# Routed experts in three split float32r terms, with weights as the moving operand

## The reference, cut to what matters

```python
scores = sigmoid(h @ gate_w.T)                       # 1024 x 16
topk_score, topk_ids = top_k(scores.T, cap)          # each of 16 experts takes cap = 128 tokens
xin = h[topk_ids]                                    # 16 x 128 x 512
up = einsum('ecd,efd->ecf', xin, up_w) + up_b[:, None, :]      # F = 2048
g  = einsum('ecd,efd->ecf', xin, gw) + gb[:, None, :]
eo = silu(g) * up
eo = einsum('ecf,edf->ecd', eo, down_w) + down_b[:, None, :]
out = zeros_like(h).at[topk_ids].add(eo * topk_score) + shared(h)
```

## Time and profile before

| | |
|---|---|
| median of 3 runs | 3031.3 us (3031.16 to 3031.32) |
| profiled execution | 3031.67 us, of which the trace's span is 3029.8 us |
| PE busy | 2971.4 us, 98% |
| DVE, ACT busy | 1830.8 us, 60%; 1361.5 us, 45% |
| last block, first to last matmul | 2335.88 to 3019.83 us |
| its step | 10.58 us |
| its DMA, 2400 to 2900 us | busy share 0.80, 306 GB/s |

### The profile page before, as it was taken

The page is one execution under the profiler, slowest core; times in us unless marked ns, Lnnn a source line. Parts: engine busy times, 40 slices in busy tenths (PEclk is TensorE's granted clock), DMA queues, the critical chain, the costliest instruction groups (busy, mean ns, idle before and its releaser), DMA issues. The chain is left out here.

```text
span 3029.8 us, 44905 instructions
## 1 busy us (share of the span) xinstructions
PE 2971.4 (98%) x15813; PEld 1762.5 (58%) x15813; DVE 1830.8 (60%) x1606; ACT 1361.5 (45%) x1888; POOL 48.2 (2%) x43
## 2 busy tenths in 40 slices
PE   8999999999899999999999999999999999999998
PEld 4888888888433333333333333355544888888886
DVE  4544444444799999999999999764664111111111
ACT  3121211211698888888898888443610111111110
POOL 0000000000000000000000000000001000000000
PEclk9999999999999999999999999999999999999999
DMA  5555555556555545454555455302051888787884
GB/s 203 183 186 189 193 188 178 189 194 191 140 129 126 131 116 133 113 133 116 123 124 126 123 126 122 100 15 70 1 212 52 303 311 309 300 310 305 305 306 173
DMA packets 230454, 518.59 MB, mean 171 GB/s; under 512 B 18114, under 2 KB 84290, under 8 KB 200764
## 3 DMA queue, kind: packets, MB, share of 16 engines
q1 hardware_dynamic: 226764, 508.79, 52.3%
q0 software_dynamic: 3584, 8.39, 1.2%
HBM read 403.66 MB, written 113.44 MB: 171 GB/s over the span
## 5 line engine op out<-in xcount | busy, mean ns | idle before, releaser
L845 DVE TENSOR_TENSOR AC<-AC,PR 128x2048 f32<-128x2048 f32 x496 | 1093.7, 2285 | 6.7 <-ACT PR L808 6.7
L808 ACT ACTIVATE PR<-PS 128x1024 f32<-128x1024 f32 x1024 | 994.0, 1023 | 144.5 <-DVE AC L845 98.3
L713 PE MATMUL PS<-QS,KS 128*128 128x512 f32 x2048 | 645.0, 436 | 18.9 <-ACTq L817 9.2
L713 PEld LDWEIGHTS PS<-QS,KS 128*128 128x128 f32 x2048 | 320.9, 189 | 549.9 <-ACT PR L808 518.8
L760 PE MATMUL PS<-PR,VC 128*32 128x512 f32 x4096 | 547.3, 606 | 1.0 <-ACT PR L808 1.0
L1694 ACT ACTIVATE SE<-PS,GB 128x128 f32<-128x128 f32 x256 | 73.1, 368 | 642.1 <-PE PS L1651 642.0
L369 ACT ACTIVATE KH<-PS,bk_s 128x512 fp32r<-128x512 f32 x128 | 88.1, 688 | 561.3 <-PE PS L420 561.3
L276 DVE SCALAR_TENSOR_TENSOR KL<-PS,bk_s,KH 128x512 fp32r<-128x512 f32 x128 | 95.7, 751 | 269.0 <-ACT KH L369 269.0
L1651 PEld LDWEIGHTS PS<-XE,EW 128*128 128x128 f32 x2048 | 233.2, 192 | 12.0 <-issue 12.0
L1651 PEld LDWEIGHTS PS<-AT,EW 128*128 128x128 f32 x2048 | 232.9, 192 | 12.5 <-issue 12.5
L1651 PE MATMUL PS<-AT,EW 128*128 128x128 f32 x2048 | 233.8, 275 | 1.7 <-DVEq L1733 1.7
(11 more groups left out here) (169 smaller groups left out, 2174.6 us busy)
## 6 DMA issues: line engine op xcount, KB each, us to landing
KS<-kh_d SPq DMA_DIRECT2D x256, 256.0 KB
EW<-in_up_w SPq DMA_DIRECT2D x64, 1024.0 KB, 4.8
EW<-in_gw SPq DMA_DIRECT2D x64, 1024.0 KB, 6.9
EW<-in_down_w SPq DMA_DIRECT2D x64, 1024.0 KB, 9.0
AT<-in_ctx SPq DMA_DIRECT2D x32, 1024.0 KB, 5.7
kh_d<-KH SPq DMA_DIRECT2D x32, 1024.0 KB, 4.4
kl_d<-KL SPq DMA_DIRECT2D x32, 1024.0 KB, 6.5
v_d<-VS SPq DMA_DIRECT2D x128, 256.0 KB, 3.0
```

The costliest lines, as they stand in the source:

```text
L713: m = pe.matmul(PS[:, 2 * slot + jj, :], KS[s][:, j, t * P:(t + 1) * P], QS[x_][:, j, :], start=True, stop=True)
L808: nc.scalar.activation(PR[t][:, 2 * hp:2 * hp + 2], PS[:, 2 * slot:2 * slot + 2, :], ACT.Exp, scale=SCALE).then_inc(s_exp, 1)
L845: v.tensor_tensor(a[:], a[:], PR[t][:], ALU.add).then_inc(s_acc, 1)
```

## The change

The routed experts are computed in the split form of the first block. Tokens (128x128 tiles of XEH, XEL) and later hidden values (HTH, HTL) are stationary, weights (WH, WL) move, 512 columns at a time. The result has tokens on partitions. So the biases can't be added by partition any more: they come in as the first matmul of each product, whose stationary operand PICK selects, out of a tile BIAS with all experts' biases in hi and lo rows, the row that belongs to the step. The hidden values have to be turned by PE before the down product. Weights arrive in a ring of six 1 MB tiles RAW; ScalarE copies each to WH, VectorE makes WL, both in a ring of five pairs. The block is written out in full, with no loops. The middle block's scratch moves to EX, its end gets the split of the first three weight tiles and of the biases, and `down(5)` moves ahead of the transposes of the chosen tokens.

```diff
+        TILES = [("g", 0), ("u", 0)]
+        for S in range(STEPS):
+            TILES += ([("g", S + 1), ("u", S + 1)] if S + 1 < STEPS else []) + [("d", S)]
+        def load_raw(sp, n):
+            kind, S = TILES[n]
+            if n >= RAWS:
+                sp.wait_ge(s_lo, n - RAWS + 1)
+            src = {"g": gw, "u": up_w, "d": down_w}[kind]
+            sp.dma_start(RAW[:, n % RAWS], src[S // FC, S % FC]).then_inc(s_raw[n % RAWS], 16)
+        def weights_hi(act, n):
+            act.wait_ge(s_raw[n % RAWS], 16 * (n // RAWS + 1))
+            if n >= PAIRS:
+                act.wait_ge(s_used, n - PAIRS + 1)
+            nc.scalar.activation(WH[n % PAIRS][:], RAW[:, n % RAWS], ACT.Copy).then_inc(s_hi, 1)
+        def weights_lo(dve, n):
+            dve.wait_ge(s_hi, n + 1)
+            nc.vector.tensor_tensor(WL3[n % PAIRS][:], RAW[:, n % RAWS], WH[n % PAIRS][:].bitcast(F32), ALU.subtract).then_inc(s_lo, 1)
...
                 down(4)
+                down(5)
                 pe.wait_ge(s_tk, 1)
                 bank = claim(pe, "topk")
...
-                down(5)
                 down(6)
...
+                act.wait_ge(s_br, 32)
+                filled(act, "u17")
+                nc.scalar.activation(PICK[:], pick[:, 0:4 * E], ACT.Copy).then_inc(s_bs, 1)
+                nc.scalar.activation(BIAS[:], BR, ACT.Copy).then_inc(s_bs, 1)
+                for n in range(EARLY):
+                    weights_hi(act, n)
...
+                def bias(bank, column, part):
+                    pe.matmul(PS[:, bank, :], PICK[:, column:column + 1].to_broadcast([P, CAP]), BIAS[:, part, :], start=True, stop=False)
+                def rows_product(kind, S, bank):
+                    e, k = divmod(S, FC)
+                    n = NTH[kind, S]
+                    bias(bank, e * FC + k, 0 if kind == "g" else 1)
+                    pe.wait_ge(s_lo, n + 1)
+                    hi, lo = WH[n % PAIRS], WL3[n % PAIRS]
+                    terms = [(x, w, c) for c in range(DC) for x, w in ((XEH, hi), (XEH, lo), (XEL, hi))]
+                    for i, (x, w, c) in enumerate(terms):
+                        m = pe.matmul(PS[:, bank, :], x[e % 2][:, c, :], w[:, c, :], start=False, stop=i == len(terms) - 1)
+                    m.then_inc(s_used, 1)
+                def turn_hidden(S):
+                    pe.wait_ge(s_hid, S + 1)
+                    if S:
+                        pe.wait_ge(s_htl, S)
+                    for f in range(FT):
+                        m = pe.transpose(PS[:, 4, f * P:(f + 1) * P], HE[S % 2][:, f * P:(f + 1) * P], ident[:])
+                    m.then_inc(s_t, 1)
+                def down(S):
...
+                    pe.wait_ge(s_htl, S + 1)
+                    terms = [(h, w, f) for f in range(FT) for h, w in ((HTH, hi), (HTH, lo), (HTL, hi))]
...
+                gate(0)
+                up(0)
+                for S in range(STEPS):
+                    if S + 1 < STEPS:
+                        gate(S + 1)
+                    turn_hidden(S)
+                    if S + 1 < STEPS:
+                        up(S + 1)
+                    down(S)
+                    if S % FC == 1 and S // FC + 1 < E:
+                        turn_rows(S // FC + 1)
...
+                for S in range(STEPS):
+                    if S % FC == 2 and S // FC + 1 < E:
+                        rows_hi(S // FC + 1)
+                    split(3 * S + PAIRS)
+                    hidden_hi(S)
+                    split(3 * S + PAIRS + 1)
+                    if S + 1 < STEPS:
+                        silu(S + 1)
+                    split(3 * S + PAIRS + 2)
...
+                for S in range(STEPS):
+                    if S % FC == 0 and S:
+                        output(S // FC - 1)
+                    if S % FC == 2 and S // FC + 1 < E:
+                        rows_lo(S // FC + 1)
+                    split(3 * S + PAIRS)
+                    hidden_lo(S)
+                    split(3 * S + PAIRS + 1)
+                    if S + 1 < STEPS:
+                        hidden(S + 1)
+                    split(3 * S + PAIRS + 2)
```

More of the change, by code:

```diff
@@ L1583, in program @@
[L1583 to L1596, removed]
+                dve.wait_ge(s_xh, 1)
@@ new lines, in _ @@
+                v.tensor_tensor(XEL[0][:], PS[:, bank, :].rearrange("p (c t) -> p c t", c=DC), XEH[0][:].bitcast(F32),
+                                ALU.subtract).then_inc(s_xl, 1)
+        s_g1, s_ga, s_gb = sem("second_gathered"), sem("tokens_gathered"), sem("last_tokens_gathered")
+        s_si, s_hid, s_t, s_hth, s_htl, s_xt, s_y, s_sc = (sem(n) for n in (
+            "expert_silu", "expert_hidden", "hidden_turned", "hidden_hi", "hidden_lo",
+            "expert_rows_turned", "expert_output", "expert_scattered"))
@@ L1598, in _ @@
+        XG = [XG0] + [AT[:, i, :] for i in range(2, 8)] + [X[:, i, :] for i in range(TT)] + [WO[:, 3, :]]
+        with nc.Block() as block:
             @block.sync
             def _(sp):
[L1600 to L1612, removed]
@@ L1655, in down @@
-                def down(e, x_, k):
-                    S = e * FC + k
-                    pe.wait_ge(s_hi, S + 3)
-                    if k == 0:
-                        pe.wait_ge(s_yb, e + 1)
-                    for f in range(FT):
-                        m = pe.matmul(PS[:, 4 + x_, :], HE[k % 2][:, f, :], WD[k][:, f, :],
-                                      start=(k == 0 and f == 0), stop=(k == FC - 1 and f == FT - 1))
-                    m.then_inc(s_dn, 1)
-                def expert(e, x_, last=False):
-                    for k in range(FC):
-                        if k + 1 < FC:
-                            up(e, x_, k + 1)
-                        elif not last:
-                            up(e + 1, 1 - x_, 0)
-                        down(e, x_, k)
-                        if k == 1 and not last:
-                            turn(e + 1, 1 - x_)
@@ L1675, in _ @@
-                pe.sem_inc(s_dn, 2)
-                up(0, 0, 0)
-                with pe.Fori(0, E // 2 - 1) as i:
-                    for x_ in range(2):
-                        expert(i * 2 + x_, x_)
-                expert(E - 2, 0)
-                expert(E - 1, 1, last=True)
+                pe.wait_ge(s_bs, 5)
+                gate(0)
[9 more added lines that the diff above has]
+                        turn_rows(S // FC + 1)
@@ new lines, in split @@
+                def split(n):
+                    if EARLY <= n < len(TILES):
+                        weights_hi(act, n)
+                for n in range(EARLY, PAIRS):
+                    split(n)
+                silu(0)
+                for S in range(STEPS):
[7 more added lines that the diff above has]
+                    split(3 * S + PAIRS + 2)
@@ L1747, in by_contraction @@
+                output(E - 1)
 def by_contraction(w):
@@ L1763, in by_blocks, with expert_biases, expert_pick @@
     return wide
+def expert_biases(gb, up_b, down_b):
+    rows = np.zeros((4, E, 2, 3, FF // 4), gb.dtype)
+    for i, b in enumerate((gb, up_b)):
+        rows[:, :, :, i] = b.reshape(E, 4, FF // 4).transpose(1, 0, 2)[:, :, None]
+    rows[0, :, :, 2] = down_b[:, None]
+    return rows.reshape(P, 3, FF // 4)
+def expert_pick():
+    rows = np.zeros((4, E, 2, 4 * E + 2), np.float32)
+    for k in range(4):
+        for e in range(E):
+            rows[k, e, :, e * 4 + k] = 1
+    rows[:, :, 0, 4 * E] = 1
+    rows[:, :, 1, 4 * E + 1] = 1
+    return rows.reshape(P, 4 * E + 2)
 def window_mask():
```

247 lines of the change are left out of this document (138 added, 109 removed).

## The result

The changed kernel takes 2934.7 us (median of 4 runs, 2931.5 to 2936.2) where the kernel before takes 3031.3 (3031.2 to 3032.5): a ratio of 0.968, with an interval of 0.966 to 0.970. The profiled execution took 2935.78 us.

A forecast was written before the change was run, and what follows sets the result against it. PE's work was taken to bound the last block: -78.0 us there, -7.0 at its start, +1.6 and -0.5 at its end, together -83.9 from 3031.67, giving 2947.8, as a median 2947 us; range 2932 to 2982.

The forecast's parts named there:

- What bounds the block: Last block: it lasts as long as PE's work, which falls from 683.9 to 605.9 us, -78.0 us.
- the distance of the float32r matmuls: Expert products of the last block: 2448 matmuls 0.2333 us apart, as in the first block, 571.1 us.
- a sign of being wrong: Last block: wrong if the float32r distance differs, or PE waits each step for HTL or a WL tile.
- unexpected 0.228: Last block: a float32r matmul distance in us that the range reaches down to, giving 2934 us.
- The forecast proper: Whole kernel: a step of 9.4 to 9.6 us in the last block and 2940 to 2955 us, given 73%.
- the rival of closer matmuls: Last block: float32r matmuls 0.2145 us apart, a step of 8.75 us, 2901 us in all; chance 5%.
- VectorE and ScalarE priced at nothing: Last block: VectorE needs 8.6 and ScalarE 7.1 us of a 9.47 us step, so PE's work covers both.
- the rival of a late VectorE: Last block: VectorE or ScalarE late, an excess of 0.1 to 0.6 us a step, 2954 to 2986 us; chance 15%.
- Transfers hidden: Last block: weight loads at 332 GB/s, some 345 with the scattered rows, land in time and cost nothing.
- Start, -7.0: Start of the last block: with down(5) moved ahead, PE begins expert products at 2328.9, 7.0 us earlier.
- End: End of the last block: PE idle 1.6 us before the last down product, +1.6; two VectorE operations become one, -0.5.
- The slower rival: Last block: matmuls with freshly written moving tiles stand 0.32 us apart, +206 us, 3153 us; chance 4%.

The follow-up runs named there:

- two-term kernel: The changed kernel without the third term (low part of tokens or hidden values by high part of weights) in all split products: 2862.4 us.

## Why the prediction was right, point by point

**What bounds the block:** right. PE is idle for 0.10 us between 2329.18 and 2922.15, and its work is the block; without its 144 bias matmuls it was shorter by 0.226 us for each. The block is 88.0 us shorter; the prediction had 76.4.

**The term that was off is the distance of the float32r matmuls.** The prediction took 0.2333 from the first block, and named a distance that differs as a sign of being wrong. The count was right, 2448. But they do not stand 0.2333 apart here: the down product's twelve, from 2602.09 to 2604.82, take 2.73 us, 0.2275 each. The trace's start times in nanoseconds resolve it: once a product has settled the distance is 226.7 ns, where the first block has 229 to 236, 233.3 on average, throughout. From a bias matmul on the first four distances are 228 to 235 ns on average, and behind the transposes it takes some eight, of 224 to 236, before they settle; in the first block they never do. Of the transposes three distances are 0.108 and the last to the bias 0.03, 0.355 together and not 0.44, but the bias matmul behind them takes 0.315 instead of 0.233, so that both together are as predicted. With these the block adds up: 595.9 less 79 x 0.355 for transposes, 79 x 0.085 for the longer bias behind them, 1.5 of waiting and 0.16 for the end of the last matmul gives 559.5 us for 2448 matmuls, 0.2286 each. 2448 x (0.2333 - 0.2286) = 11.5 us is nearly the whole of the miss of 12. The prediction carried its range down to an "unexpected 0.228", and that is where the time fell: no reason was known for it, so that the range held is in part luck. The forecast proper, a step of 9.4 to 9.6 us and 2940 to 2955 us, did not hold; the step is 9.31.

What sets 0.2333 in the one block and 0.2267 in the other stays open. Not the bias (taken out: the mean is still 0.229) and not the order of the terms. More work on ScalarE and VectorE beside it doesn't go with the longer distance: with VectorE busy 446 of 500 us this block is the faster one, and the first, at 47%, the slower. The 0.2145 of the rival of closer matmuls was an estimate, half of a float32 record's 0.429 us (3.43 us for the 8 of a down product). No run shows it: the shortest distance inside a product of this block is 0.224 us, and 0.223 in the experiments.

**VectorE and ScalarE priced at nothing:** right, with more room than was thought. VectorE waits for the hi part 79 times in the 64 steps, 61 us in all, where the prediction had a wait of 1.2 us in each; it is VectorE that waits. The limit of VectorE is 8.2 us a step, by the two-term kernel, not 8.6. So the rival of a late VectorE starts 0.4 us later than it was put, and PE's step, (595.9 - 1.5) / 64 = 9.29 us, leaves it 1.1 us. The subtraction took 2287 ns, as said, and a group by line gives it:

```profile
L906 DVE TENSOR_TENSOR WL<-RAW,WH 128x2048 fp32r<-128x2048 f32 x192 | 436.4, 2287 | 61.0 <-ACT WH L901 60.9
L901 ACT ACTIVATE WH<-RAW 128x2048 fp32r<-128x2048 f32 x192 | 361.9, 1913 | 4.8 <-DMA RAW<-in_gw 2.1
```

**Transfers hidden:** right. 345 GB/s were expected and 347 are moved; landing takes less than before:

```profile
DMA to landing us min/median/max: 4.8/6.0/9.2
```

**Start, -7.0:** right, 6.7 between the two profiles and 7.5 by the experiment that moves down(5) back. From the first shared down product on, the stretch went from 126.7 to 119.4 us, 7.3; the other 0.6 were lost ahead of it. The 0.429 us for a record of the shared down products, 3.43 us by 8, was about right: the 32 behind the small transposes take 13.83 us (2312.85 to 2326.68), 0.432 each.

**End:** the wait before the last down product was put at 1.6 and is 1.5. Behind the last matmul 0.5 was expected and 1.1 came. Two VectorE rows became one, and the sum counted their durations only: from the first of them to the scatter it was 3021.90 - 3019.87 = 2.03 us, and now it is 2926.18 - 2925.16 = 1.02, for the handover between the two is gone as well.

**The slower rival**, matmuls 0.32 apart as in the earlier trace rows, did not come, though the moving tiles are freshly written here too. Such a distance does show behind the first matmul after the transposes or after idle time (2598.78 to 2599.09 above, 0.315), once and not on every matmul.

## What to carry to other kernels

When one engine fills a block, its count of instructions by a distance read from a like block of the same kernel gave this block's time to 2% and the kernel's to 0.4%; the same shape differed by up to 3% between two blocks of one kernel (0.2333 and 0.2267), so that with thousands of them the distance is the term that needs a range. To ask whether a second engine still fits, count its instructions from start to start and not by their durations, which here overstated VectorE's step by 0.4 of 8.2 us. Packing small matmuls onto row groups has a price on the way in and out: a single pair between full matmuls lost 0.40 us there and saved 0.23. Whether more of them together would pay was not run.

## What the runs showed of the hardware

GpSimd's scatters take twice as long beside the new work of VectorE. The group by line after, and that of the kernel before under it:

```profile
L1668 POOL DMA_INDIRECT out<-YO,token x16 | 51.8, 3240 | 514.8 <-DVE YO L1813 514.8
```

```profile
L1629 POOL DMA_INDIRECT out<-YO,token x16 | 24.9, 1555 | 643.8 <-DVE YO L1729 602.3 <-issue 41.5
```

The mean of 3.24 us hides two values. VectorE subtracts for 3 x 2.28 us of each step of 9.31. 15 scatters took 3.35 to 3.41 us, and each of them started 0.36 us into a subtraction; the last one stands behind the last subtraction and took 1.55, as in the kernel before. The last two scatters:

```profile
2895.47 3.35 POOL L1668 DMA_INDIRECT out<-YO,token  x1 [33.77 <-DVE YO L1813]
2926.18 1.55 POOL L1668 DMA_INDIRECT out<-YO,token  x1 [27.37 <-DVE YO L1813]
```

At the last one the other engines and the loads have stopped as well, but in the kernel before scatters amid PE's work and 306 GB/s of transfers took 1.55 us. The first scatter of the kernel with two terms was not slow either:

```profile
2368.39 1.92 ACT L901 ACTIVATE WH<-RAW 128x2048 fp32r<-128x2048 f32 x1 [1.75 <-DMA RAW<-in_gw]
...
2369.90 1.62 POOL L1668 DMA_INDIRECT out<-YO,token  x1 [6.99 <-DVE YO L1813]
...
2370.34 2.29 DVE L906 TENSOR_TENSOR WL<-RAW,WH 128x2048 fp32r<-128x2048 f32 x1 [0.71 <-ACT WH L901]
2371.03 1.91 ACT L901 ACTIVATE WH<-RAW 128x2048 fp32r<-128x2048 f32 x1 [0.24 <-DMA RAW<-in_up_w]
```

It took 1.62 us beside ScalarE's copies and 403 GB/s of transfers (2360 to 2380 us), with a subtraction that started 0.44 us behind it; the next 14 started 0.36 or 0.37 us into one and took 3.35 or 3.36. So it is a subtraction under way at the scatter's start that goes with the longer time; by what mechanism, no run here shows. It costs nothing in the changed kernel: GpSimd waits 514.8 us for YO beside it, and the scatter that ends the kernel is one of 1.55 us.
